# Vision tower on one core: attention weights fetched a stage ahead, one scaling for two norms, first image normalised early, mixer over 576 rows

## The reference

```python
def _performer(x, ...):                      # a1: 147 features, a2: 576
    h = _ln(x, n1g, n1b)
    kqv = h @ kqvw + kqvb                    # 64 keys, 64 queries, 64 values
    k, q, v = split(kqv)
    kp, qp = _prm_exp(k, wrand), _prm_exp(q, wrand)   # 32 random features
    D = einsum('btm,bm->bt', qp, kp.sum(1))
    kptv = einsum('btd,btm->bdm', v, kp)
    y = einsum('btm,bdm->btd', qp, kptv) / D
    y = v + (y @ projw + projb)
    return y + gelu(_ln(y) @ w1 + b1) @ w2 + b2

t = _unfold(x, 7, 4, 2)      # 32 images, 1024 tokens of 147 features
t = _performer(t, *a1)
t = _unfold(t, 3, 2, 1)      # 256 tokens of 576 features
t = _performer(t, *a2)
t = _unfold(t, 3, 2, 1)      # 64 tokens
h = t @ proj_w + proj_b      # and a class token ahead: 65 x 192 an image
```

## Time and profile before

| what | value |
|---|---|
| median of 3 runs | 1901.69 us (1900.58 to 1902.76) |
| the profiled execution's own time | 1902.59 us |
| its span, first to last instruction | 1900.9 us |
| mean granted TensorE clock over the span | 0.898 of full speed |
| TensorE matmuls | 1572.1 us busy, 83% of the span |
| VectorE, ScalarE, POOL | 1093.1, 817.5, 736.5 us busy |
| DMA | 163.95 MB, mean 86 GB/s |

### The profile page before, as it was taken

One profiled execution on the slowest core, in us unless ns is written; L12 is line 12 of the kernel. 1 busy time (PEld: TensorE's weight loads), 2 busy tenths in 40 slices (PEclk: granted clock), 3 DMA queues, 4 the chain that ended last, 5 costly groups with the idle time before them and its releaser, 6 DMA issues. The chain is left out here.

```text
span 1900.9 us, 35054 instructions
## 1 busy us (share of the span) xinstructions
PE 1572.1 (83%) x11224; PEld 1215.6 (64%) x11225; DVE 1093.1 (58%) x3263; ACT 817.5 (43%) x1651; POOL 736.5 (39%) x680
## 2 busy tenths in 40 slices
PE   3879999977999985896987889994598577766997
PEld 2667777756888863675766779994476233355554
DVE  2678898856677633497486613232701699942332
ACT  0457777742555533182264533331355333324221
POOL 2547677731222213342433024441200499920232
PEclk9999999988999976897988779997699799967999
DMA  3243433323334222000000634443400766535331
GB/s 63 45 94 75 79 76 77 77 63 96 104 110 117 79 60 73 1 2 14 1 2 18 166 127 176 172 169 84 99 1 13 196 162 157 137 87 137 99 96 44
DMA packets 219797, 163.95 MB, mean 86 GB/s; under 512 B 116340, under 2 KB 199343, under 8 KB 219173
## 3 DMA queue, kind: packets, MB, share of 16 engines
q1 hardware_dynamic: 206783, 146.99, 29.3%
q0 software_dynamic: 6528, 14.19, 2.7%
q10 hardware_dynamic: 6374, 1.33, 0.4%
HBM read 106.10 MB, written 32.35 MB: 73 GB/s over the span
## 5 line engine op out<-in xcount | busy, mean ns | idle before, releaser
L2234 POOL TENSOR_TENSOR ssm_scan_prod<-ssm_scan_S,ssm_crep 128x1056 f32<-128x1056 f32 x48 | 159.3, 3320 | 144.6 <-DVE ssm_scan_S L2251 144.6
L1279 PE MATMUL a_psum<-a2w_W,a_hT 128*128 128x256 f32 (+1 forms) x640 | 149.1, 380 | 5.4 <-DVE a_z L1071 4.5
L755 PE MATMUL a_psum<-a_W,a_hT 126*128 126x256 f32 x512 | 134.9, 396 | 0.0
L1279 PEld LDWEIGHTS a_psum<-a2w_W,a_hT 128*128 128x128 f32 (+1 forms) x640 | 118.6, 190 | 20.6 <-issue 6.5
L2275 PE MATMUL ssm_scan_psum<-ssm_ST,ssm_EW 112*128 112x512 f32 (+1 forms) x288 | 106.3, 508 | 22.4 <-PEq L1986 20.4
L2251 DVE TENSOR_TENSOR_SCAN ssm_scan_S<-ssm_scan_X,ssm_scan_psum 128x1056 f32<-128x1056 f32 x48 | 113.0, 2354 | 4.4 <-ACT ssm_scan_psum L2263 0.2
L2891 ACT ACTIVATE moe_tiles_GT<-moe_tiles_psum,moe_tiles_mine 128x128 f32<-128x128 f32 x240 | 66.4, 376 | 111.4 <-PE moe_tiles_psum L2842 111.4
L2275 PEld LDWEIGHTS ssm_scan_psum<-ssm_ST,ssm_EW 112*128 112x128 f32 x288 | 52.5, 196 | 90.9 <-issue 69.9
L755 PEld LDWEIGHTS a_psum<-a_W,a_hT 126*128 126x128 f32 x512 | 90.6, 192 | 30.6 <-issue 21.9
L543 POOL TENSOR_TENSOR a_rstd<-a_rstd,a_mhalf 128x8 f32<-128x8 f32 x64 | 105.1, 1642 | 5.0
L2263 ACT ACTIVATE ssm_scan_psum<-ssm_scan_psum 128x1056 f32<-128x1056 f32 x48 | 49.7, 1035 | 119.9 <-PE ssm_scan_psum L2275 119.9
(11 more groups left out here) (692 smaller groups left out, 4038.2 us busy)
## 6 DMA issues: line engine op xcount, KB each, us to landing
ssm_scan_grep<-gains SPq DMA_DIRECT2D x48, 528.0 KB, 4.7
moe_tiles_mine<-moe_W SPq DMA_DIRECT2D x40, 579.0 KB, 3.1
a2w_X<-t SPq DMA_DIRECT2D x192, 96.0 KB
t<-a_O SPq DMA_DIRECT2D x128, 64.0 KB
xrows<-in_x SPq DMA_DIRECT2D x30, 192.0 KB
glu_tiles_mine<-glu_W1r SPq DMA_DIRECT2D x24, 234.5 KB, 3.1
a_X<-xrows SPq DMA_DIRECT2D x60, 91.9 KB, 3.0
a_PX<-t SPq DMA_DIRECT2D x96, 48.0 KB
```

Of the source, the lines that this page charges most:

```text
L755: last = nc.tensor.matmul(KQ[q][:, j, :], hT[0:MAIN, q, PARTS * j:PARTS * j + PARTS], W[0:MAIN, :], start=False, stop=True)
L1279: last = nc.tensor.matmul(KQ[:, j, :], hT[i % 2][0:rows, k, PARTS * j:PARTS * j + PARTS], W[0:rows, k, :], start=(k == 0), stop=(k == 4))
L2234: nc.gpsimd.tensor_tensor(prod[n % 2][:], S[n % 2][:], crep[:, cols], ALU.mult).then_inc(s_prod, 1)
```

## The change

There are five parts. No output of the program is computed otherwise than by the reference's formulas.

1. **First image in the preparation.** H, R, the statistics' tiles, the mask and v1 are allotted ahead of a1_prep. `statistics`, `aggregate` and `scale` are functions that both blocks can call; image 0's calls stand in a1_prep, and POOL's memsets for the main block go there too. TensorE's wait for the weights' DMAs is taken directly on their semaphore `s_w`, no longer on `s_ready`, which SyncE raised after it had issued ten more DMAs.
2. **Mixer over 576 rows.** The last piece of `KT` is 63 features and the ones; the 576th feature of a normed row is minus the sum of the others, and a fourth hop of `Later` folds its weights into the other rows with two matmuls (constants lessall, lastmix). The last piece of two tiles stands side by side in hR, so that one transposition turns two of them, and its products are taken as four matmuls of 64 rows at the head of `matmuls(i, 0)`, in two pairs on the upper and the lower half of the array.
3. **Attention weights ahead.** A class `AttentionWeights` holds raw weights and biases. The first attention's are loaded in step 4 of `tokens`, the second's in at_images. Only the output projection's weights and bias are fetched in the stage. The twins are gone (the copies out of PSUM are made twice instead, for 64 rows each), and oT's row of ones is a POOL memset behind the roots.
4. **One scaling for two norms.** With v the variance of a row of h_a, both norms together are a subtraction of the mean and a product with one inverse root, of (1+eps) w - eps, where w is the variance plus eps. xn comes from h_a straight away; h_b, still needed later, is made by `keep`, four rows' tiles after each chunk of q and k.
5. **Scopes.** `patches`, and `tokens` apart from it, get a `cleanup_on_exit` of their own, and the first attention's weights one around both: eight where there were five up to the experts. A tile lP of the attention is dropped for lE.

The diff, cut:

```diff
+        else:
+            pe.wait_ge(self.s_clear, 14)
+            pe.wait_ge(self.s_wt, 2)
+            nc.tensor.matmul(ps[:, two:two + 256], self.lessall[:], self.W[0:EMB + 1, 4, :], start=True, stop=True)
+            nc.tensor.matmul(ps[:, two + 256:two + 512], self.lastmix[:].rearrange("p a b -> p (a b)"), self.W[0:EMB + 1, 4, :], start=True, stop=True).then_inc(self.s_feat, 1)
...
             nc.vector.tensor_copy(self.W[:, 0:4, 3 * EMB:], ps[:, three:three + 8 * FEATS].rearrange("p (k f) -> p k f", k=4))
-            nc.vector.tensor_copy(self.W[0:65, 4, 3 * EMB:], ps[0:65, three + 8 * FEATS:three + 10 * FEATS])
...
                 sp.wait_ge(s_w, 16 * NW)
-                sp.sem_inc(s_ready, 1)
...
+                pool.wait_ge(s_wide, 2)
+                scale(pool, 0, 0)
...
+                statistics(dve, 0, 0)
+                aggregate(dve, 0)
...
-                pe.wait_ge(s_ready, 1)
+                pe.wait_ge(s_w, 16 * NW)
...
+                if live(t) and not (isinstance(t, int) and t == 0):
+                    scale(pool, t, p)
...
-        hN, hT = pair("hN", [PARTS, tiles, width]), pair("hT", [PARTS, 5, BANK])
+        hN, hR, hT = pair("hN", [PARTS, tiles, main]), pair("hR", [PARTS, tiles, EMB]), pair("hT", [PARTS, 5, BANK])
...
+                if t == 4:
+                    ahead(sp)
...
                 wait(dve, s["t2"], i - 1)
                 for j in range(tiles):
-                    last = nc.vector.tensor_scalar(hN[i % 2][:, j, 0:dim], X[i % 2][:, j, :], mv[i % 2][:, j, 0:1], rstd[i % 2][:, j:j + 1],
-                                                   ALU.subtract, ALU.mult)
+                    nc.vector.tensor_scalar(hN[i % 2][:, j, :], X[i % 2][:, j, 0:main], mv[i % 2][:, j, 0:1], rstd[i % 2][:, j:j + 1],
+                                            ALU.subtract, ALU.mult)
+                for j in range(tiles):
+                    last = nc.vector.tensor_scalar(hR[i % 2][:, 2 * (j % 2) + j // 2, 0:EMB - 1], X[i % 2][:, j, main:dim - 1], mv[i % 2][:, j, 0:1],
+                                                   rstd[i % 2][:, j:j + 1], ALU.subtract, ALU.mult)
                 last.then_inc(s["norm"], 1)
 
             def exponent(i):
...
-                c0, rows = KT[k]
-                for j in range(tiles):
-                    last = nc.tensor.transpose(ps[0:rows, TB[k] * BANK + PARTS * j:TB[k] * BANK + PARTS * j + PARTS], hN[i % 2][:, j, c0:c0 + rows], ident[:])
+                for j in range(tiles if k < 4 else tiles // 2):
+                    frm = hN[i % 2][:, j, PARTS * k:PARTS * k + PARTS] if k < 4 else hR[i % 2][:, 2 * j:2 * j + 2, :].rearrange("p t c -> p (t c)")
+                    last = nc.tensor.transpose(ps[:, TB[k] * BANK + PARTS * j:TB[k] * BANK + PARTS * j + PARTS], frm, ident[:])
                 last.then_inc(s[f"t{k}"], 1)
 
             def matmuls(i, j):
@@ -1275,8 +1310,13 @@
                     for k in range(5):
                         pe.wait_ge(s[f"th{k}"], i + 1)
                     wait(pe, s["z"], i)
-                for k, (_, rows) in enumerate(KT):
-                    last = nc.tensor.matmul(KQ[:, j, :], hT[i % 2][0:rows, k, PARTS * j:PARTS * j + PARTS], W[0:rows, k, :], start=(k == 0), stop=(k == 4))
+                    for h in range(2):
+                        for u in range(2):
+                            p0 = EMB * u
+                            nc.tensor.matmul(KQ[:, h + 2 * u, :], hT[i % 2][p0:p0 + EMB, 4, PARTS * h:PARTS * h + PARTS], W[p0:p0 + EMB, 4, :],
+                                             start=(h == 0), stop=False, skip_group_check=True)
+                for k in range(4):
+                    last = nc.tensor.matmul(KQ[:, j, :], hT[i % 2][:, k, PARTS * j:PARTS * j + PARTS], W[:, k, :], start=False, stop=(k == 3), skip_group_check=True)
...
+                sp.dma_start(rawo[:], dram(*wts.weight("o", 0), [(DIM, HALF), (HALF * DIM, 2), (1, DIM)])).then_inc(s_w, 16)
...
-                sp.wait_ge(s_w, 16 * n)
-                sp.sem_inc(s_b, 1)
...
                 pe.wait_ge(norm.ident_done, 2)
-                pe.wait_ge(s_b, 1)
-                pe.wait_ge(s_twin, 2)
+                wts.arrived(pe)
...
-                norm.ones(act, oT)
-                act.wait_ge(s_b, 1)
-                nc.scalar.copy(raw[:, 0:4, DIM:], raw[:, 0:4, PARTS:DIM]).then_inc(s_twin, 1)
-                nc.scalar.copy(raw[0:EMB, 4, DIM:], raw[0:EMB, 4, PARTS:DIM]).then_inc(s_twin, 1)
+                wts.arrived(act)
...
+                nc.scalar.copy(W[:, 0, 0:4 * PARTS].rearrange("p (b c) -> p b c", c=PARTS), turned[:, :, 0, :]).then_inc(s_ts, 1)
+                for p0 in (0, EMB):
+                    nc.scalar.copy(W[p0:p0 + EMB, 1, 0:4 * PARTS].rearrange("p (b c) -> p b c", c=PARTS), turned[0:EMB, :, 1, :]).then_inc(s_ts, 1)
...
+                    if second:
+                        norm.keep(dve, norm.PER * c, norm.PER * (c + 1))
...
+                def _(sp):
+                    ahead(sp)
...
-        for r in range(self.rounds):
-            pool.wait_ge(self.moment, 7 * (r + 1))
+        pool.wait_ge(self.moment, 7 if self.raw is None else 8)
+        for n, out in ((2, self.rstd),) if self.raw is None else ((3, self.rstd), (2, self.rstd1)):
             for a, b in self.PIECES:
-                self.nc.gpsimd.tensor_tensor(self.rstd[:, a:b], self.tmp[:, 2, a:b], self.mhalf[:, a:b], ALU.pow).then_inc(self.root, 1)
...
+            nc.vector.tensor_scalar(tmp[:, 3, :], tmp[:, 2, :], 1.0 + EPS, -EPS, ALU.mult, ALU.add).then_inc(self.moment, 1)
+        if meanwhile:
+            meanwhile()
...
+    def keep(self, dve, a, b):
+
+        dve.wait_ge(self.root, 2 * len(self.PIECES))
+        for i in range(a, b):
+            self.nc.vector.tensor_scalar(self.rows[:, i, :], self.raw[:, i, :], self.tmp[:, 0, i:i + 1], self.rstd1[:, i:i + 1], ALU.subtract, ALU.mult)
...
+            with nc.cleanup_on_exit(), ExitStack() as ctx2:
+                atw = AttentionWeights(nc, ctx2, "atw", first, False)
+                with nc.cleanup_on_exit(), ExitStack() as ctx3:
+                    later = Later(nc, ctx3, t1, under("L0_tok_a2_", performer_names), a["L0_tok_proj_w"], a["L0_tok_proj_b"])
+                    with nc.cleanup_on_exit():
+                        patches(nc, "a1", a["x"], xrows, t1, under("L0_tok_a1_", performer_names), later)
+                    with nc.cleanup_on_exit():
+                        tokens(nc, later, t2, h0, a["cls_tok"], h_a, stats_b, atw.load)
                 with nc.cleanup_on_exit():
-                    attention(nc, "at", None, None, h_a, stats_b, stats_a, first, False, fetch)
-                with nc.cleanup_on_exit():
-                    attention(nc, "fa", None, h_a, h_b, stats_a, stats_b, second, True)
-                with nc.cleanup_on_exit():
-                    experts(nc, "moe", h_b, h_a, None, stats_b, stats_a, xs, ys, moe, False, early)
+                    attention(nc, "at", None, h_a, stats_b, stats_a, first, atw, False, fetch, faw.load)
+            with nc.cleanup_on_exit():
+                attention(nc, "fa", h_a, h_b, stats_a, stats_b, second, faw, True)
+            with nc.cleanup_on_exit():
```

More of the change, by code:

```diff
@@ L156, in tensor @@
             last.then_inc(self.s_turn, 1)
-        else:
+        elif hop == 2:
             pe.wait_ge(self.s_wt, 1)
@@ L423, in patches @@
         xd = st.sbuf("xd", [PARTS, tiles, 2])
-        v1 = [st.sbuf(f"v1{p}", [PARTS, tiles, EMB + 1]) for p in range(2)]
         z = st.sbuf("z", [PARTS, 2, tiles, FEATS])
@@ L873, with tokens @@
 TILE, NTILE = 104, 20
-def tokens(nc, later, dst, h0, cls, rows, known):
+def tokens(nc, later, dst, h0, cls, rows, known, ahead):
     tiles, steps, width = 4, IMAGES // 2, 577
-    dim, COLS = 576, 256
+    dim, main, COLS = 576, 512, 256
     KT = later.KT
@@ L1428, in attention @@
+def attention(nc, name, raw, rows, known, stats, w, wts, second, fetch=None, ahead=None):
     HG = 6
@@ L1515, in _ @@
                 norm.roots(pool)
+                pool.wait_ge(norm.root, len(norm.PIECES) * (2 if second else 1))
+                nc.gpsimd.memset(oT[HALF:HALF + 1, :, :], 1.0)
                 pool.wait_ge(s_own, 2)
```

326 lines of the change are left out of this document (175 added, 151 removed).

## The result

The changed kernel takes 1875.64 us in the median of 4 runs (1873.76 to 1881.96), before 1901.94 (4 runs): a ratio of 0.9847 with a 95% interval of 0.9826 to 0.9868 on record (the two medians alone give 0.986). It is faster by 26 us where 40 were forecast, and its median lies 1.6 us over the upper end of the range. The profiled executions are 1873.96 and 1902.59, their spans 1872.2 and 1900.9, so the traces to be compared differ by 28.7.

The account below looks back on a forecast made before the run. TensorE's instruction sum was taken to bound the second mixer, waits the other places; -13.3 - 14.6 + 0.85 - 6.9 - 6.6 + 1.3 - 1 = -40.3 us, from 1902.59 profiled to a forecast 1861, range 1852 to 1874.

Parts of the forecast that it names:

- Start: First mixer: earlier weight products and image 0's early H bring the first exponent from 53.83 to 40.7 or earlier: -13.3 us.
- Second mixer: Sixteen steps with cheaper products and fewer transposes: -14.6 us, against +0.85 for VectorE's longer norming.
- VectorE has 43 of 125 us idle there, so I count it once: Second mixer: VectorE's norming grows 0.85 us a step, charged only where the first step waits: +0.85 us.
- the second rival: Second mixer: VectorE's 0.85 falls in the step's chain; the mixer saves 2.4, program 1872; chance 0.1.
- TensorE's own saving: Second mixer, each step: 0.75 us from half-height products and 0.22 from two fewer transposes.
- The premise: Second mixer's steady part: TensorE, busy 123.29 of 125 us, sets the time by the sum of its instructions.
- The change of height: Second mixer's 64-row products: no cost beyond the factor; the pair in the rows leaves at most 0.1 us a change.
- First attention: Preparation: weight transposes no longer await the weights' copies, so the turn of the rows comes at 732.4: -6.9 us.
- Scopes: Three more cleanups at 0.4 us each, rounded up: +1.3 us, ends 1.2 and 3.3.
- Clock: Attention preparations: waits at TensorE's low clock level shorten by more than the work: -1 us, ends -3 and +2.
- a mixer saving 2.6: Third rival: second mixer's 64-row halves run one after the other, or drain; program 1873; chance 0.08.
- a step is still over 15.3 us: Second mixer: sign that the prediction is wrong, against a forecast step of 14.7 us.

Follow-up runs that it names:

- With the stores moved: Changed kernel with the first mixer's two border stores two images later in SyncE's queue: 1872.05 us, ratio 0.983.
- the copy first in both kernels: VectorE's copy a_PO moved ahead of the second mixer's norming, in the changed kernel (1874.61 us, 0.9844) and in the kernel before (1.0009).
- the run of before with the copy first: Kernel before with only VectorE's copy a_PO moved ahead of the norming: step 15.32 us, ratio 1.0009.
- the step at full height: Changed kernel with the last piece's four products over all 128 rows, output not the reference's: step 15.21 us, program 1879.12 us (0.9866).
- the last run: Changed kernel with border stores late, copy a_PO first, h's store on ScalarE's queue and the rows' fetch a step later: 1872.21 us (0.9831).

## Why the prediction was right and wrong

- **Start, 13.3 forecast, 10.8 measured at the exponent.** The chain was right up to 27.9. The failed term is image 2's landing: "the queue sets it ... lands at 38.3 to 38.9". It was priced with the 4.9 us of a load in a quiet queue, behind stores of 520 KB; it took 7.0, from an issue 0.8 later than forecast, and its reader started at 41.28. With the stores moved the reader starts at 39.30. Of the 10.8, 9.1 are left at the first mixer's last exponent (395.18 to 386.12), 10.4 at the end of its last store's issue (428.73 to 418.29), and 9.5 at the second mixer's opening: 0.9 went into the new scope's cleanup. The fourth hop cost nothing: its last copy ends at 418.31, beside that store.
- **Second mixer, 13.75 forecast, 5.5 measured.** The failed step is "VectorE has 43 of 125 us idle there, so I count it once". VectorE's idle share was real and irrelevant: between G's product (L1342, now L1382) and TensorE's turn of the patches there is a chain through VectorE's a_O, POOL's inverse root (the norming waited 0.98 us for it, in both kernels), VectorE's norming and its copy a_PO. Its length went from 5.92 to 6.74 us, by 0.82. TensorE's three other groups gave 3 x 0.433 = 1.30. 1.30 less 0.82 is 0.48, and the step fell by 0.48. This is near the second rival's mechanism, at a smaller price than it was given (a mixer that saves 2.4): the rival set the 0.85 against nearly all that TensorE saves, where inside that part nothing that TensorE saves or loses counts. Two steps of the changed kernel also waited for a_PX, 2.2 us in all.
- **TensorE's own saving** was mis-sized beside it. With the copy first in both kernels, a step falls from 15.32 to 14.74, by 0.58 and not by 0.75 + 0.22 = 0.97. Missing are about 0.08 in the half-height products, 0.20 in the rows beside them, 0.03 in the transpositions, and 0.10 in the patch projection (L1407), whose ten records take 1.73 at full height too, for 1.63 before; why, no run shows. That this run's 14.74 is the forecast's 14.7 is luck: it has the 0.34 in it that VectorE held already before.
- **The premise, "there the sum of TensorE's instructions is the time",** was off too, by the 0.34 us a step that the run of before with the copy first recovered. Over the eight steps in 125 us that is 2.7, more than the 1.7 that the busy time of 123.29 leaves: a record's modelled end covers the start of a gap, so the row says 0.15 idle where the starts say 0.32 over the pace. The earlier trace rows leave out L1299 and L1356, so the gap stood in none of their rows.
- **The change of height.** The prediction put at most 0.05 to 0.1 on it. The runs show 0.10 in the row ahead and 0.10 in the row behind, beside 1.06 for 0.98 in the products. Against four times 0.216, the 1.06 has 0.20 of it as well: about 0.2 going in and 0.2 coming out, 0.4 a step. The earlier trace rows held part of it unseen: the first full-height record there is followed after 0.454 us where the next two take 0.349, so the 1.49 that the factor 0.54 was taken from was 0.10 too long. The Trainium skill, "TensorEngine Tiling (Array Packing)", Key Properties, says that a change of mode drains TensorE; the trace agrees, with these 0.2 us a change. Where it stood, most of it fell into the part that VectorE held: the step at full height is 15.21 for 15.18. The same page of the Trainium skill says that tiles run in parallel; the trace agrees, with two records in the time of one, in both orders.
- **First attention, 6.9 forecast, 6.8 measured; second, 6.6 and 6.1.** Right, and so was the mechanism: the second's two chains were nearly tied, within 1.5 us and not 0.4. In the other trace of the unchanged attentions (before, copy first) the turns stand 11.7 and 18.1 us behind the openings, for 12.3 and 18.0, so the first attention's gain is known to about 0.6. The first attention's edit and the start's were not undone by themselves; their gains are read off the traces.
- **Scopes, 1.3 forecast; 0.9, 0.1 and 0.3 by the ledger.** The sum is right, but the cost is not one price. The clearing of semaphores alone took 0.46 us at 420.2, then 0.39 and 0.09 ahead of the first attention, where the kernel before cleared once, for 0.89.
- **Clock, 1 forecast.** No event isolates it. Behind the second turn the ledger has 1.2, in stages that took 999.9 to 1010.2 us in the fourteen traces, so it says nothing. The 20 scalings of `keep` don't show either: from that turn to the experts' opening it is 141.0 us, 139.6 and 141.2 in the two traces without them.
- **The range** took in a mixer saving 2.6 with all else right (1873), but not that with the start's shortfall beside it. The measured 1875.64 is both at once; they were given as alternatives. And the sign "a step is still over 15.3 us" was set so far from the forecast 14.7 that 15.18 passed under it with more than half of the mixer's gain gone.

What stays open: why the steady part of the first mixer keeps only 9.1 of the 10.8 us; what the remaining 6.2 us of waits for a_PX in the last run are; and the 0.10 in L1407. Removing the added scopes was not tried.

## What to carry to other kernels

A busy share of 98% or 99% does not say that an engine's sum is the step. Take one step and subtract start from start: a gap of a few tenths, behind which the next instruction starts right at another engine's end, points to a chain. Work added to that chain costs its full length, whatever the other engine's idle share is, as long as the chain is the longer of the two. Price a load by what is ahead of it in the queues at its new place, not by how long it took at its old one. Where two chains into one instruction are nearly tied, make both edits or neither.

## What was not expected of the hardware

- Executions of one kernel differ, in part with the mean granted TensorE clock over the span. The kernel before took 1897.35 us at 0.901 and 1912.22 at 0.891, but both 1897.43 and 1909.3 at 0.898; the changed one took 1873.76 at 0.900 and 1881.96 at 0.895. A change of 2 us needs the step's length, not the program's time.
- Half-height records of 256 columns run two at a time, a new two every 0.216 us where full ones follow singly at 0.216, in either order of the halves. A change of height costs about 0.2 us, half of it in the rows on the other side of the change.
- 520 KB of stores ahead of a load, half of them in pieces of 256 bytes, lengthened not only its landing but its issue: 4.35 us for four DMAs, 2.81 without them.
